# GpSimd's products of the expert stage wait for VectorE's last product instead of for the search's first count

## The reference, cut to what matters

```python
xt = x.reshape(-1, Dx)                                   # 4096 tokens, 128 features
router_scores = jax.nn.softmax(xt @ Wr + br, axis=-1)    # 64 experts
# routing:
order = jnp.argsort(-router_scores, axis=0)
sorted_vals = jnp.take_along_axis(router_scores, order, axis=0)
group_score = sorted_vals.reshape(Tq, G, En).sum(axis=1) # G = 64, Tq = 64
_, top_flat = jax.lax.top_k(group_score.reshape(-1), Tq * K)   # K = 16
...
fs = where(mask, router_scores, 0); fs = fs / (fs.sum(axis=-1, keepdims=True) + 1e-06)
up = jnp.einsum('td,edh->teh', xt, Wup) + bup
gate = jnp.einsum('td,edh->teh', xt, Wgate) + bgate
h = jax.nn.silu(up) * gate * fs[:, :, None]
out = jnp.einsum('teh,ehd->td', h, Wdown) + fs @ bdown
```

## Time and profile before

| what | us |
|---|---|
| median of 3 runs | 1144.07 (1143.19 to 1144.93) |
| the profiled execution, time | 1143.17 |
| the profiled execution, span of its instructions | 1141.1 |
| DVE busy in the span | 790.5 |
| PE busy in the span | 884.4 |
| POOL busy in the span | 128.9 |
| POOL's 33 products (L1156) | 44.9 |

### The profile page before, as it was taken

One profiled execution on the slowest core, in us unless ns is written; L12 is line 12 of the kernel. 1 busy time (PEld: TensorE's weight loads), 2 busy tenths in 40 slices (PEclk: granted clock), 3 DMA queues, 4 the chain that ended last, 5 costly groups with the idle time before them and its releaser, 6 DMA issues. The chain is left out here.

```text
span 1141.1 us, 20063 instructions
## 1 busy us (share of the span) xinstructions
PE 884.4 (78%) x7220; PEld 498.4 (44%) x7220; DVE 790.5 (69%) x1453; ACT 440.5 (39%) x788; POOL 128.9 (11%) x107
## 2 busy tenths in 40 slices
PE   5428999999898766999784719999987974575774
PEld 4116766666565442333231303434435832343442
DVE  0762344688878894999977657888874433899982
ACT  3515666656545333554354620111112264222221
POOL 3420000000000001000005720000000000232232
PEclk8858999999989877999997969999998886787787
DMA  7400000000000000555342347666630000000000
GB/s 187 71 1 2 2 3 2 3 2 3 2 2 2 2 1 37 194 202 185 144 151 109 130 122 238 203 201 200 205 110 1 1 1 0 1 4 15 9 19 28
DMA packets 53988, 79.80 MB, mean 70 GB/s; under 512 B 14288, under 2 KB 28432, under 8 KB 53776
## 3 DMA queue, kind: packets, MB, share of 16 engines
q1 hardware_dynamic: 49520, 76.57, 21.2%
q10 hardware_dynamic: 4384, 2.10, 0.6%
HBM read 40.90 MB, written 35.65 MB: 67 GB/s over the span
## 5 line engine op out<-in xcount | busy, mean ns | idle before, releaser
L1485 PE MATMUL bank<-ex_hh,Wd 128*128 128x512 f32 x256 | 130.3, 601 | 6.7 <-DVE ex_hh L1546 6.7
L1171 ACT ACTIVATE so_u<-bank,bu 128x512 f32<-128x512 f32 x128 | 87.5, 686 | 84.3 <-PE bank L57 84.2
L1546 DVE TENSOR_TENSOR ex_hh<-ex_pg,bank 128x512 f32<-128x512 f32 x128 | 84.4, 674 | 33.4 <-PE bank L1471 16.1
L882 ACT ACTIVATE att_qk<-bank 128x512 f32<-128x512 f32 x128 | 66.8, 602 | 45.2 <-PE bank L712 44.7
L970 DVE TENSOR_TENSOR att_am<-bank,causal 128x512 f32<-128x512 f32 x64 | 44.1, 688 | 50.2 <-PE bank L746 50.1
L746 PE MATMUL bank<-att_qk 64*128 64x128 f32 x1024 | 78.0, 294 | 0.0
L746 PEld LDWEIGHTS bank<-att_qk 64*128 64x128 f32 x1024 | 65.5, 196 | 20.6 <-issue 20.6
L1279 DVE SCALAR_TENSOR_TENSOR so_made<-bank,bg,so_u 128x512 f32<-128x512 f32 x95 | 69.5, 754 | 6.9 <-DMA hidden<-so_made 5.1
L1485 PEld LDWEIGHTS bank<-ex_hh,Wd 128*128 128x128 f32 x256 | 47.9, 192 | 57.0 <-issue 32.7
L1471 PE MATMUL bank<-F,spread 128*128 (+1 forms) x128 | 48.2, 387 | 23.6 <-PEq L122 23.6
L1156 POOL TENSOR_TENSOR so_made<-so_u,so_g 128x512 f32<-128x512 f32 x33 | 44.9, 1396 | 177.0 <-DVE so_cnt L1334 170.2
(11 more groups left out here) (376 smaller groups left out, 1847.6 us busy)
## 6 DMA issues: line engine op xcount, KB each, us to landing
hidden<-so_made SPq DMA_DIRECT2D x128, 256.0 KB, 2.0
ex_pg<-hidden SPq DMA_DIRECT2D x64, 512.0 KB, 4.1
xin<-in_L_attn_x_dram ACTq DMA_DIRECT2D x8, 256.0 KB, 7.0
out_dram<-ff_ot SPq DMA_DIRECT2D x8, 256.0 KB, 2.3
so_other<-so_key SPq DMA_DIRECT2D x2, 512.0 KB, 5.5
wm<-in_L_wmod_dram SPq DMA_DIRECT2D x2, 384.0 KB, 5.0
F<-so_fhi SPq DMA_DIRECT2D x2, 256.0 KB, 4.4
F<-so_flo SPq DMA_DIRECT2D x2, 256.0 KB, 5.7
```

Source lines behind the costliest of these rows:

```text
L882: nc.scalar.activation(qk[t % 2][:, r, :, :].rearrange("p a l -> p (a l)"), psF[r], ACT.Relu).then_inc(s_["fe"], 1)
L1171: nc.scalar.activation(u[m % NU_][:], psU[m % 3][:, :], ACT.Silu, bias=bu[:, k:k + 1], scale=1.0 / WS).then_inc(s_u, 1)
L1485: nc.tensor.matmul(psY[j][:, :], Wd[:, n, :], hh[n % 4][:], start=False, stop=n == EBLK - 1).then_inc(s_dn[n % 4], 1)
L1546: nc.vector.tensor_tensor(hh[k % 4][:], pg[k // 2 % 4][:, k % 2, :], psW[k % 4][:, :], ALU.mult).then_inc(s_hh[k % 4], 1)
```

## The change

One wait of POOL, ahead of its loop of products, is on another semaphore. `s_cnt` reaches FIRST + 1 when DVE has finished the count of round 0 (L1334). `s_made` reaches FIRST + BY_DVE when DVE has made its last product, item 94. No instruction is added, removed or moved in any engine's list.

```diff
                         assert step.n == N_MASKS
 
-                        pool.wait_ge(s_cnt, FIRST + 1)
+                        pool.wait_ge(s_made, FIRST + BY_DVE)
                         for m in range(BY_DVE, ITEMS):
                             pool.wait_ge(s_g, FIRST + m - BY_DVE + 1)
                             pool.wait_ge(s_store[m % NM], 16 + 16 * (m // NM))
```

## The result

The changed kernel takes 1151.06 us (median of 20 runs, 1143.88 to 1155.22); the kernel before, run beside it, 1140.69 us (median of 20, 1135.96 to 1145.13). The ratio is 1.0085 with a 95% interval of 1.0064 to 1.0105: slower by 9.7 us (7.3 to 12.0 us); the two medians alone lie 10.4 us apart. The forecast was 8.6 us longer, from 1144.07 to 1152.7. The profiled executions are 1143.17 us before and 1152.45 after.

A forecast was written before the change was run, and what follows sets the result against it. DVE's chain was taken to set the end of the route stage. Merge contention of 9.0 us less 0.4 us gained in the rounds gave 8.6 us longer, 1144.07 to 1152.7 us; range 1149.0 to 1155.0.

The forecast's parts named there:

- What bounds the kernel: Route stage: DVE's chain sets the end, so every us it grows or shrinks goes to the end.
- Start and number of products: POOL starts at 589.9 instead of 611.4 and makes no more than nine products before round 0.
- Term 2: Merge: nine POOL products take turns with DVE's two-input instructions, 1.007 us each, making DVE's chain 9.0 us longer.
- Rival (a): Merge: fewer turns, none between back-to-back DVE instructions; five turns, 4.6 - 0.4 = 4.2 us longer, 1148.3; chance 0.10.
- Rival (b): Merge: full blocking, each product holds DVE for its own 1.31 us; 11.4 us longer, 1155.5; chance 0.10.
- Rival (c): Merge: no contention in this form, or POOL still held; only the rounds' gain is left, 1143.7; chance 0.06.
- Term 1: Rounds: with POOL ahead, DVE waits less for PE's sums; 0.4 us gained, bounds nothing to 3.4 us.
- rival (d): Merge free of POOL, clock rises early, rounds give their whole excess of 3.4 us; 1140.7; chance 0.02.
- Term 3: The rest: factors' part keeps its 6.4 us loss; remaining stage and all later ones shift as a block.
- The sum: Whole kernel: 9.0 - 0.4 = 8.6 us longer, from 1144.07 to 1152.7.

The follow-up runs named there:

- two buffers: Kernel before plus nine POOL multiplications of two different spent buffers from item 94, real products late; with and without waits between them: 1154.11 and 1149.64 us, one run each.
- memsets: Kernel before plus nine POOL writes of zeros over a spent buffer from item 94 on, real products late as before; ratio 1.0039 (1.0008 to 1.0070).
- copies: Kernel before plus nine POOL copies of one spent buffer to another from item 94 on, real products late; ratio 1.0076 (1.0045 to 1.0108).
- one buffer twice: Kernel before plus nine POOL multiplications of one spent buffer by itself from item 94 on, real products late; ratio 1.0095 (1.0061 to 1.0128).
- The kernel with 12 ahead: Against the kernel before: POOL starts when the merge is done, PE issues 12 items ahead of round 0 instead of 9, swap at n == 22; ratio 0.9953.
- the four kernels with 12 ahead: Kernel before with POOL from merge end, AHEAD 12; IN_ROUNDS 12, 16 (swap at 29), 16 (swap at 28), 14: ratios 0.9953, 0.9964, 0.9935, 0.9933.
- 16 in the rounds with the swap at 29: Kernel before with POOL from merge end, 12 items ahead, IN_ROUNDS 16, swap at n == 29, only item 127 behind it; ratio 0.9964 (0.9941 to 0.9988).

## Why the prediction was right, point by point

**What bounds the kernel.** Right. All that the merge lost went to the end of the stage, less what the rounds gave back.

**Start and number of products.** Right. The first product started 1.84 us behind L1313 (forecast 1.6), and exactly nine fell in the merge.

**Term 2, 9.0 us.** Right in mechanism and size. The 1.007 us read from L1382 held for the merge: 3.27 for L1314, 2.17 and 2.28 for the halves, 1.22 for the last pair, 9.0 us in all. The turns that were read from the earlier trace rows are what made the number nine instructions and not five; as a rule for every DVE instruction, "neither engine has two in a row" is too strong, since L1364 had to let two more products by, above. Rival (a) fell with the first pair, where both halves are long. Rival (b), 1.31 us each, fell by the same rows: part of a product's own time lies beside DVE's turn. Rival (c) fell too. The section "Who interferes with whom" of "SBUF — State Buffer" in the Trainium skill agrees with the runs on who is held: writes of POOL not, reads yes, reductions with one input not. What it says of fully blocking the other engine for a whole instruction stands there for VectorE's 2-port mode; for the two-input instructions of this merge the runs show less than that, 1.0 us of a product's 1.25 to 1.31.

**Term 1, 0.4 us.** Mis-sized; it measured 1.7. The step that failed is "if the clock rises as long after PE's return as before". POOL's lead is worth 0.5, as worked out, and measured so where the clock came back as late as before. The other 1.2 is the clock: in the changed kernel it came back 3.5 us behind the first sum and not 6.1. That the sooner clock does this without the lead too, the two kernels with two buffers show (3.8 and 3.7 us, 1.1 to 1.2 us gained). I had taken its place as given, and named an earlier rise only in rival (d), as an effect that I held for unlikely. Why it came back sooner stays open, as the table above shows.

**Term 3.** Right as to the route: from `v` to L1391 the same 27.2 us. `v` itself came 0.3 us later, from the transfer. That the rest "shifts as a block" is not what the profiles show: from the second L1391 to the end of the span it is 469.9 to 475.6 us in kernels that are the same there.

**The sum.** In the profiles the route costs 7.7 us; 9.0 - 0.4 had been 8.6, so two errors of 1.3 and 0.3 stand against each other, and with rounding that is the 7.7. By the runs it is 9.7 (7.3 to 12.0), in which both 7.7 and 8.6 lie. The time itself was 1151.06, only 1.6 us below the 1152.7, and that closeness is luck: the base was taken from three runs at 1144.07 where twenty have 1140.69, 3.4 us too high, and the medians then lay 10.4 us apart and not 8.6, 1.8 us the other way. From the base of twenty runs the forecast would have been 1149.3.

**What stays open.** The whole times of the kernels with extra POOL operations exceed what their route explains by 4 to 5 us (memsets: +4.5 of the whole, +0.2 of the route; copies +8.7 and +3.3; one buffer twice +10.9 and +6.7). For the last two 3.4 and 3.5 us of it are seen in the profile, below; no run tells why these kernels should draw it more often, or whether it is chance. Open too are what brings the clock back early in the rounds, why one buffer read twice costs less than two, and when L1364 gets its turn.

## What to carry to other kernels

An idle engine is not a free one: before work is moved to GpSimd beside VectorE, list VectorE's instructions in the new place by how many SBUF inputs each has, and count one delay for each pair of a two-input instruction and a GpSimd product that meets. An instruction with one SBUF input isn't safe by that alone: the reductions were, the quick TENSOR_SCALAR wasn't. The price can be read in advance from any place where the two already meet, as here from one line whose usual and longest executions differed by 1.007 us. Where GpSimd's work must overlap, put it beside reductions and instructions that read PSUM. The kernel with 12 ahead did so and was 7.2 us shorter on the route; 1.8 us of that is the tail with three products fewer, the rest an earlier swap and shorter rounds.

## What the runs showed of the hardware

How long one GpSimd operation of 128 x 512 float32 puts back a VectorE instruction with two SBUF inputs: a memset 0, a copy 0.35 us, a product of one buffer with itself 0.78, a product of two buffers 1.0. I had not expected the third to differ from the fourth. A TENSOR_SCALAR with one SBUF input that runs at twice the pace of a reduction is held as well, up to 3.95 us instead of 1.28 beside a queue of products; in each of the four kernels with 12 ahead it ended 1.08 us behind the end of one of POOL's products, once only after two further products had gone ahead of it.

The whole time of one kernel moves by over 10 us between runs (before: 1135.1 to 1145.8), more than most effects here. It goes with PE's mean granted clock, which was 0.888 in the quickest of these runs and 0.876 in the slowest, and the profiles show stages far from the change where that differs. In one profile the attention stage has its clock at 0.86 from 90 to 100 us and reaches L1313 at 582.5; in another at 0.56, and L1313 at 588.3. Stretches of 10 us, first of the kernel with copies, then of the kernel before:

```profile
90.00:100.00 10.00, 9.27 (x155) 6.60 (x149) 1.81 (x3) 4.98 (x10) 0.00 (x0) 0.86 0.01 2
```

```profile
90.00:100.00 10.00, 9.77 (x122) 7.52 (x114) 1.81 (x3) 4.34 (x8) 0.00 (x0) 0.56 0.01 2
```

Both kernels have the same instructions up to there. Likewise in the second layer's attention, where PE works without a pause at the low level for 10 us in nine of the fourteen profiles, for 14 in one, and for 17 in four (copies, one buffer twice, two buffers, and 16 in the rounds with the swap at 29). These four have 473.4 to 475.6 us from the second L1391 to the end of the span, the ten others 469.9 to 472.0. A part of the 17 us in the kernel with two buffers:

```profile
903.00:908.00 5.00, 5.00 (x26) 5.00 (x26) 1.70 (x4) 0.58 (x1) 0.00 (x0) 0.50 0.00 0
908.00:913.00 5.00, 5.00 (x20) 3.97 (x20) 1.03 (x3) 0.78 (x2) 0.00 (x0) 0.50 0.00 0
913.00:918.00 5.00, 5.00 (x21) 4.40 (x21) 1.73 (x4) 1.17 (x2) 0.00 (x0) 0.50 0.00 0
```

So a difference of a few us between two kernels of this size is read from the same stretch of both profiles, not from their whole times.
